# Graph layer on one core: the broadcast table of destination indices loaded as 16-bit instead of 32-bit numbers

## The chip, the cores and the metric

The kernel runs on one core of a Trainium2 chip. A core has five engines that run their own instruction streams and meet only at semaphores: TensorE (PE, with its weight loads shown as PEld), VectorE (DVE), ScalarE (ACT), GpSimd (POOL) and SyncE (SP), and 16 DMA engines that all queues share. The metric is the device time of one execution in microseconds (us); lower is better.

## The reference, cut to what matters

50,000 nodes with 160 features each, 50,000 edges sorted by destination node. For each edge the source node's features are gathered, put through a linear layer, multiplied by weights that a small network makes of the edge's own features, and added up per destination node. The sums turn the node's own linear layer by an angle; then comes a layer norm.

```python
h = silu(edge_scalars @ fc_w1 / sqrt(8));  weight = h @ fc_w2 / sqrt(64)
gs, gv = f_s[edge_src], f_v[edge_src]
m0a = gs * ys * w1_;                 m0b = sum(gv * yv[:, None, :], -1) * INV3 * w4_
m1a = gs[..., None] * yv[:, None, :] * w2_[..., None];  m1b = gv * ys[..., None] * w3_[..., None]
mid = segment_sum(edge_feat, edge_dst, num_segments=N) / sqrt(16)
angle = 0.1 * (mid_s @ lin3_w) / sqrt(96) * node_attr
return layernorm(x + cos(angle) * scfeat + sin(angle) * conv)
```

## The kernel before

Edges and nodes are padded to 392 tiles of 128 (`NT`), that is 196 pairs of tiles (`NPAIR`). The program has two stages, each a hand-written order per engine.

**Edge stage.** One step per pair. POOL gathers the source rows with an indirect DMA per tile (`gather`, L316), 644 bytes for each of 128 partitions, into a ring of 48 pairs. PE transposes them (L480) and runs the linear layers, ACT copies PSUM to SBUF, DVE forms the messages. `lin2` is applied per edge (L440, L442), and the rows of a tile that have the same destination are summed by a matmul with a 0/1 matrix `same_sb` (`combine`, L423 and L427). ACT copies the sums to a ring of 48 pairs, `comb_sb` (L553). POOL adds them to the table `acc` in HBM, one accumulating indirect DMA per tile (`scatter`, L329): 392 of them. Two semaphores, `scattered[0]` and `scattered[1]`, serve the even and the odd tile of a pair, and a scatter first waits until the scatter of the same parity in the pair before has landed (L328), so at most two are in flight and POOL's instructions behind that wait stand too.

POOL's order is written out: 120 gathers (`2 * AHEAD`), then for each tile one scatter and 0.73 gathers on average (272 over 372 scatters, L344), so one or two gathers stand among any two consecutive scatters' slots; the last 20 scatters have none.

**The table in question.** `same_sb` is made on DVE in L689, two instructions per pair. One takes a row of 256 destination indices (this tile's 128 and the next tile's, the same on all partitions), compares each with the partition's own destination index, `dst_f`, and multiplies by a weight matrix of fp32. The rows lie in `dstrow_sb`, in two rounds of 9 rows of 128 indices. One load per 4 pairs (`load_rows`, L542, on ACT's DMA queue) fills a round: each of the 128 partitions gets the same 9 x 128 indices of `dst_rows` from HBM. There are 49 loads. ACT issues load c after it has copied the last tile of the chunk before (L573), and DVE waits for it once in 4 pairs (L685).

```python
dstrow_sb = sb("dstrow_sb", [P, ROUNDS, 2 * CHUNK + 1, P], i32)
act.dma_start(dstrow_sb[:, c % ROUNDS, :, :], rows.to_broadcast([P, 2 * CHUNK + 1, P])
              ).then_inc(dstrow_in[c % ROUNDS], 16)
```

On the same ACT queue `load_scalars` (L535) brings 32 KB per chunk. On SP's queue, 50 stores of zeros to `acc` run in the first 125 us, and five loads of the node stage's inputs (L243, L255) go out between 892 us and 1133 us.

**Node stage.** When both `scattered` semaphores are full (L277), SP loads `acc` back and the node stage runs: `x_n` tiles, self connection on PE, angle, y and layer norm on POOL, DVE and ACT, stores on SP.

Of the kernel before, what the change touches and what calls it, by code (L numbers as in the profile page):

```python
# [6 lines left out]
P = 128  # L7
# [15 lines left out]
CHUNK = 4  # L23
ROUNDS = 2
# [26 lines left out]


def gnn_program(nc, xa, x_odd, x_last, src, dst, dst_rows, ea4, ea8t, constants, acc, out):
    fp32, i32 = mybir.dt.float32, mybir.dt.int32
    ALU, ACT = mybir.AluOpType, mybir.ActivationFunctionType
    NT = dst.shape[1]
    NPAIR = NT // 2
# [32 lines left out]
    with ExitStack() as ctx:  # L90
        def sb(name, shape, dt=fp32):
            return ctx.enter_context(nc.sbuf_tensor(name, shape, dt))
# [23 lines left out]
        row_sb = sb("row_sb", [P, NT], i32)  # L116
        dst_i = row_sb
        is_last = sb("is_last", [P, NT])
        dstrow_sb = sb("dstrow_sb", [P, ROUNDS, 2 * CHUNK + 1, P], i32)

        CS_COLUMNS = LOADED * BATCH * G * ROWA
        shared = sb("shared", [P, CS_COLUMNS + Y_RING * G * ROW])
# [811 lines left out]
def layouts(x, src, dst, edge_attr_4, edge_attr_8, node_vec1, sc_w0, sc_w1, lin1_w0, lin1_w1, fc_w1,  # L934
            fc_w2, lin2_w0, lin2_w1, lin3_w, tiles):

    n, e = x.shape[0], src.shape[0]
    rows = tiles * P
    f32 = np.float32
    xa = np.zeros((rows, ROWA), f32)  # L940
    xa[:n, 0], xa[:n, 1:1 + NV], xa[:n, 1 + NV:] = node_vec1[:, 0], x[:, NS:], x[:, :NS]
    src_p = np.zeros(rows, np.int32)
    src_p[:e] = src
    dst_p = np.full(rows, n, np.int32)
    dst_p[:e] = dst
    ea4 = np.zeros((rows, 4), f32)
    ea4[:e] = edge_attr_4
    ea8 = np.zeros((rows, EDGE_S), f32)
    ea8[:e] = edge_attr_8

    def by_component(w, rows_grouped, cols_grouped):

        u, c = w.shape
        m = np.zeros((u, 3, c, 3), f32)
        for d in range(3):
            m[:, d, :, d] = w
        if rows_grouped:
            m = m.transpose(1, 0, 2, 3).reshape(3 * u, c, 3)
        else:
            m = m.reshape(3 * u, c, 3)  # L960
        if cols_grouped:
            m = m.transpose(0, 2, 1)
        return np.ascontiguousarray(m.reshape(3 * u, 3 * c))

    lin2_a = np.zeros((P, NS + 1 + MU), f32)
    lin2_a[:NS, :NS] = lin2_w0[:NS]
    lin2_a[:NS, NS] = lin3_w[:NS, 0]
    lin2_a[NS:, NS + 1:] = lin2_w1[:NS]
    lin2_b = np.zeros((P, OUTW), f32)
    lin2_b[:NV, :NV] = by_component(lin2_w1[NS:], True, False)  # L970
    lin2_b[NV:, NV:ROW] = lin2_w0[NS:]
    lin2_b[NV:, ROW] = lin3_w[NS:, 0]
    sc_a = np.zeros((P, ROW), f32)
    sc_a[:NV, :NV] = by_component(sc_w1, False, False)
    sc_a[NV:, NV:] = sc_w0[:P - NV]
    lin1_a = np.zeros((P, ROW), f32)
    lin1_a[:NV, NS:] = by_component(lin1_w1, False, True)
    lin1_a[NV:, :NS] = lin1_w0[:P - NV]

    def two_tiles(w):  # L980

        m = np.zeros((2 * w.shape[0], 2 * w.shape[1]), f32)
        m[:w.shape[0], :w.shape[1]] = m[w.shape[0]:, w.shape[1]:] = w
        return m

    order = np.arange(P)
    values = {
        "fc_w1": two_tiles(fc_w1),
        "fc_w2": np.concatenate([fc_w2, fc_w2]),
        "lin1_a": lin1_a,  # L990
        "lin1_b": two_tiles(lin1_w0[P - NV:]),
        "lin2_a": lin2_a,
        "lin2_b": lin2_b,
        "sc_a": sc_a,
        "sc_b": np.concatenate([two_tiles(sc_w0[P - NV:])] * 2),
        "ident": np.eye(P, dtype=f32),
        "weight": np.concatenate([np.triu(np.ones((P, P))), np.full((P, P), HANDED)], axis=1).astype(f32),
    }
    constants = np.concatenate([np.pad(values[name], ((0, P - shape[0]), (0, 0)))
                                for name, shape in CONSTANTS.items()], axis=1)  # L1000
    return {
        "xa": xa,

        "x_odd": np.concatenate([xa[:, 1 + P:], xa[:, 1:1 + P], xa[:, :1]], axis=1),

        "x_last": np.ascontiguousarray(xa[:, 1 + P:]),
        "src": src_p.reshape(P, tiles),
        "dst": dst_p.reshape(P, tiles),
        "dst_rows": np.concatenate([dst_p.reshape(P, tiles).T, np.full((1, P), -1, np.int32)]),
        "ea4": ea4.reshape(P, tiles, 4),  # L1010
        "ea8t": np.ascontiguousarray(ea8.reshape(P, tiles // 2, 2, EDGE_S).transpose(1, 2, 3, 0)
                                     ).reshape(tiles // 2, 2 * EDGE_S, P),
        "constants": constants,
    }
# [21 lines left out]
```

How the kernel before makes its waits and increments, by code:

```python
def wait(eng, sem, count):  # L47
    if count > 0:
        eng.wait_ge(sem, count)
# [167 lines left out]
        @block.sync  # L218
        def _(sp):
            sp.dma_start(src_sb[:, :], src).then_inc(src_in, 16)
            sp.dma_start(constants_sb[:, :], constants).then_inc(consts, 16)
            sp.wait_ge(zeroed_tile, 1)
            for c in range(ZEROS):
                wait(sp, acc_zeroed[c % ZEROING], c // ZEROING * 16)
                sp.dma_start(acc_z[c, :, :], zeros[:, :]).then_inc(acc_zeroed[c % ZEROING], 16)
            for z in range(ZEROING):
                sp.wait_ge(acc_zeroed[z], 16 * len(range(z, ZEROS, ZEROING)))
            def ring_free(columns):
                pairs = min(NPAIR, NPAIR - X_RING + -(-columns // (2 * ROWA)))
                sp.wait_ge(xt_ready, pairs)
                sp.wait_ge(q_done, pairs)
# [1 line left out]
            def load_x_last(b):  # L236
                g, count = BATCHES[b]
                if b < LOADED:
                    ring_free((b + 1) * BATCH * G * (ROW - P))
                else:
                    over, groups = BATCHES[b - LOADED]
                    sp.wait_ge(xnt_ready, over + groups)
                sp.dma_start(xl_sb[:, b % LOADED, 0:count * P], batch_rows(x_last, b).rearrange("p j c -> p (j c)")
                             ).then_inc(xl_in[b % LOADED], 16)
# [19 lines left out]
            def store(s):  # L264
                sp.wait_ge(norm_done, s + 1)
                if s >= TAIL_FIRST:
                    sp.wait_ge(norm_pool, s + 1 - TAIL_FIRST)
                if s >= TAIL_MIDDLE:
```

## Time and profile before

| | us |
|---|---|
| median of 3 runs (lowest, highest) | 1580.86 (1576.93, 1584.43) |
| the profiled execution's own time | 1580.58 |
| its span, first to last instruction | 1578.8 |
| edge stage, to the last scatter | 0 to 1294 |
| node stage, from SP's first load of `acc` | 1296 to 1578.8 |

| engine | busy us | share of the span |
|---|---|---|
| POOL | 1293.4 | 82% |
| PE | 1284.8 | 81% |
| DVE | 932.0 | 59% |
| ACT | 816.2 | 52% |

How to read the rows: a timeline row gives the start, the duration, the engine, the line of the program, the operation and the tiles, and in brackets how long the engine stood idle before it and what ended that. A POOL row of an indirect DMA is the time in which POOL writes the descriptors; the transfer follows. POOL shows about 0.30 us between any two of these instructions, whatever they wait for, so only what is above 0.30 is a stall, and the releaser named beside 0.30 means nothing. Queue q0 in the DMA tables is POOL's own, q10 is ACT's, q1 is SP's, and q8 and q14 fetch instructions.

### The profile page before, as it was taken

How to read it: one execution, taken by the hardware profiler on the slowest of the kernel's cores; microseconds unless marked ns; L12 is line 12 of the kernel's file. 1: busy time of each engine (PE TensorE's matmuls, PEld its weight loads, DVE VectorE, ACT ScalarE, POOL GpSimd, SP SyncE). 2: the span in 40 equal slices, each digit the busy share in tenths (PEclk: the TensorE clock that was granted, in tenths of full speed). 3: DMA queues.
4: the chain of work that ended last, by engine and by line, in shares of the span. 5: the costliest groups of instructions: out<-in, count | busy, mean ns of one | idle time of the engine just before them, and what ended most of it. 6: DMA issues, size and time to landing. Idle time of an engine off the chain costs nothing. (4 is left out here: it accounts for less than half of the span.)

```text
span 1578.8 us, 28888 instructions
## 1 busy us (share of the span) xinstructions
PE 1284.8 (81%) x8524; PEld 1134.3 (72%) x8524; DVE 932.0 (59%) x4681; ACT 816.2 (52%) x1877; POOL 1293.4 (82%) x1054
## 2 busy tenths in 40 slices
PE   6999999999999777776777777777777828888884
PEld 5888888888888666666666666666666716777774
DVE  4777777777776444435444435344444407999998
ACT  3666666666665333333333333333333403988896
POOL 7777888878878877778888888778788769999997
PEclk9999999999999888888888888888888868999998
DMA  9994444444444444344444454444444449999984
GB/s 370 380 387 131 81 81 83 81 80 82 82 79 82 73 75 65 63 67 81 66 67 66 85 85 84 64 66 80 104 66 66 62 90 385 367 415 399 401 337 182
DMA packets 114761, 235.19 MB, mean 149 GB/s; under 512 B 17264, under 2 KB 77232, under 8 KB 111024
## 3 DMA queue, kind: packets, MB, share of 16 engines
q0 software_dynamic: 75264, 64.68, 28.8%
q1 hardware_dynamic: 27936, 136.82, 21.8%
q10 hardware_dynamic: 11408, 31.84, 6.0%
q8 instruction: 72, 1.18, 0.3%
q14 instruction: 81, 0.66, 0.1%
HBM read 135.88 MB, written 97.40 MB: 148 GB/s over the span
## 5 line engine op out<-in xcount | busy, mean ns | idle before, releaser
L329 POOL DMA_INDIRECT acc<-shared,row_sb x392 | 625.1, 1595 | 144.5 <-issue 97.5
L716 DVE TENSOR_TENSOR shared<-shared 128x192 f32<-128x192 f32 x196 | 70.4, 359 | 559.1 <-ACT shared L581 559.1
L480 PE MATMUL XTZ<-constants_sb,x_shared 128*128 128x128 f32 x588 | 118.9, 316 | 200.5 <-DMA x_shared<-x_odd,src_sb 194.9
L316 POOL DMA_INDIRECT x_shared<-xa,src_sb x196 | 201.5, 1028 | 60.5 <-issue 44.5
L316 POOL DMA_INDIRECT x_shared<-x_odd,src_sb x196 | 199.5, 1018 | 59.7 <-issue 48.8
L480 PEld LDWEIGHTS XTZ<-constants_sb,x_shared 128*128 128x128 f32 x588 | 66.7, 152 | 230.3 <-DMA x_shared<-x_odd,src_sb 216.5
L440 PE MATMUL OC<-constants_sb,shared 128*128 128x193 f32 x784 | 231.8, 382 | 0.0
L589 ACT COPY shared<-XTZ 128x384 f32<-128x384 f32 x196 | 93.7, 478 | 257.3 <-PE XTZ L480 257.3
L423 PE MATMUL OC<-shared 128*128 128x161 f32 x784 | 199.0, 339 | 2.8 <-ACT shared L553 2.1
L553 ACT ACTIVATE shared<-OC,is_last 128x161 f32<-128x161 f32 x392 | 154.9, 395 | 72.2 <-PE OC L427 35.6
L427 PE MATMUL OC<-shared 128*128 128x161 f32 x782 | 189.9, 328 | 0.0
L568 ACT COPY shared<-OC 128x386 f32<-128x386 f32 x196 | 94.3, 481 | 177.7 <-PE OC L442 177.7
L689 DVE SCALAR_TENSOR_TENSOR shared<-dstrow_sb,dst_f,constants_sb 128x256 f32<-128x256 int32 x392 | 173.3, 478 | 0.0
L619 ACT ACTIVATE shared<-shared,shift,rstd_mean 128x160 f32<-128x160 f32 x361 | 158.3, 513 | 17.1 <-DVE shift L861 17.0
L442 PEld LDWEIGHTS OC<-constants_sb,shared 128*128 128x128 f32 x784 | 165.6, 223 | 0.0
L442 PE MATMUL OC<-constants_sb,shared 128*128 128x97 f32 x784 | 160.1, 291 | 0.0
L468 PE MATMUL W<-constants_sb,shared 64*128 64x192 f32 x784 | 157.9, 351 | 0.0
L440 PEld LDWEIGHTS OC<-constants_sb,shared 128*128 128x128 f32 x784 | 147.8, 225 | 0.0
L427 PEld LDWEIGHTS OC<-shared 128*128 128x128 f32 x782 | 145.8, 214 | 0.0
L459 PE MATMUL FPT<-constants_sb,shared 128*128 128x160 f32 x784 | 141.3, 303 | 0.6 <-ACT shared L589 0.6
L423 PEld LDWEIGHTS OC<-shared 128*128 128x128 f32 x784 | 135.3, 216 | 4.2 <-issue 1.8
L383 POOL TENSOR_TENSOR shared<-shared,x_shared 128x640 f32<-128x640 f32 x98 | 129.7, 1324 | 0.0
(92 smaller groups left out, 2695.5 us busy)
## 6 DMA issues: line engine op xcount, KB each, us to landing
acc<-xnt_zeros SPq DMA_DIRECT2D x50, 644.0 KB, 6.7
out<-shared SPq DMA_DIRECT2D x97, 320.0 KB, 10.2
x_shared<-xa SPq DMA_DIRECT2D x13, 2254.0 KB, 11.1
shared<-acc SPq DMA_DIRECT2D x13, 2254.0 KB, 16.1
dstrow_sb<-dst_rows ACTq DMA_DIRECT2D x49, 576.0 KB, 4.2
acc<-shared,row_sb POOLq DMA_INDIRECT x392
x_shared<-x_last SPq DMA_DIRECT2D x13, 448.0 KB, 11.2
x_shared<-xa,src_sb POOLq DMA_INDIRECT x196, 3.0
```

The costliest lines, as they stand in the source:

```text
L316: pool.indirect_dma_start(out=x_sb[:, slot, j * ROWA:(j + 1) * ROWA], out_offset=None, in_=(xa, x_odd)[j], in_offset=bass.IndirectOffsetOn ...
L329: pool.indirect_dma_start(out=acc, out_offset=bass.IndirectOffsetOnAxis(ap=row_sb[:, t:t + 1], axis=0), in_=comb_sb[:, k % RING, j, :], in ...
L423: last = nc.tensor.matmul(out_rows, same_sb[:, e % SLOTS, j, 0:P], feat_sb[:, e % SLOTS, j, 0:ROWA], start=True, stop=t == 0)
L427: last = nc.tensor.matmul(out_rows, same_sb[:, b % SLOTS, i, P:2 * P], comb_sb[:, b % RING, i, :], start=False, stop=True)
L440: nc.tensor.matmul(OUT[:, o:o + OUTW], pt_sb[:, d % 2, (2 + j) * P:(3 + j) * P], lin2_b_sb[:, :], start=True, stop=False)
L442: last = nc.tensor.matmul(OUT[:, o + NV:o + OUTW], pt_sb[:, d % 2, j * P:(j + 1) * P], lin2_a_sb[:, :], start=False, stop=True)
L459: nc.tensor.matmul(F[:, j * ROW:(j + 1) * ROW], xt_sb[:, k % 2, j * P:(j + 1) * P], lin1_a_sb[:, :], start=j == 0, stop=False)
L468: last = nc.tensor.matmul(W[:, j, 0:NW], h_sb[j * NS:(j + 1) * NS, k % 2, :], fc_w2_sb[j * NS:(j + 1) * NS, :], start=True, stop=True)
L480: last = nc.tensor.transpose(XT[:, b * P:(b + 1) * P], x_sb[:, x_slot(a), column:column + P], ident_sb[:, :])
L553: nc.scalar.activation(comb_sb[:, e % RING, j, :], COMB[:, j * ROWA:(j + 1) * ROWA], ACT.Copy, scale=is_last[:, t:t + 1]).then_inc(comb_co ...
L619: last = nc.scalar.activation(y[:, j, :], y[:, j, :], ACT.Identity, bias=shift[:, k % STAGED, n:n + 1], scale=rstd_mean[:, k % STAGED, 0, ...
L689: last = nc.vector.scalar_tensor_tensor(same_sb[:, d % SLOTS, j, :], dstrow_sb[:, chunk % ROUNDS, r:r + 2, :].rearrange("p b e -> p (b e)" ...
```

## The change

The host hands over only the low 16 bits of each destination index, and the SBUF tile and its load are 16-bit. All indices are at most 50,000 and thus fit; the filler row of -1 becomes 65,535, which no index equals. The comparison L689 reads a 16-bit operand now; its output and its other operands stay fp32. A load moves 2304 bytes per partition instead of 4608, and `dstrow_sb` takes 4608 bytes of SBUF per partition instead of 9216. No instruction is added, removed or moved on any engine.

```diff
-    fp32, i32 = mybir.dt.float32, mybir.dt.int32
+    fp32, i32, u16 = mybir.dt.float32, mybir.dt.int32, mybir.dt.uint16
...
-        dstrow_sb = sb("dstrow_sb", [P, ROUNDS, 2 * CHUNK + 1, P], i32)
+        dstrow_sb = sb("dstrow_sb", [P, ROUNDS, 2 * CHUNK + 1, P], u16)
...
-        "dst_rows": np.concatenate([dst_p.reshape(P, tiles).T, np.full((1, P), -1, np.int32)]),
+        "dst_rows": np.ascontiguousarray(np.ascontiguousarray(np.concatenate([dst_p.reshape(P, tiles).T, np.full((1, P), -1, np.int32)])).view(np.uint16)[:, ::2]),
```

## Rows read from the trace of the kernel before

**Rows 1.** Busy time by stretch: PE, PEld, DVE, ACT, POOL, clock, DMA share, GB/s.

```profile
157.00:300.00 143.00, 143.00 (x1043) 127.63 (x1040) 102.62 (x535) 90.06 (x208) 116.33 (x85) 1.00 0.47 81
300.00:500.00 200.00, 200.00 (x1456) 178.24 (x1455) 142.91 (x748) 126.27 (x292) 159.63 (x117) 1.00 0.48 84
500.00:700.00 200.00, 147.04 (x873) 132.35 (x871) 87.53 (x456) 75.91 (x175) 159.13 (x118) 0.85 0.43 68
1296.00:1578.00 282.00, 226.56 (x1639) 188.20 (x1639) 249.53 (x1139) 219.06 (x503) 264.80 (x262) 0.95 0.89 356
```

**Rows 2.** POOL's instruction groups from 157 to 1296 us: busy, mean ns, idle before.

```profile
L329 POOL DMA_INDIRECT acc<-shared,row_sb x392 | 625.1, 1595 | 144.5 <-issue 97.5 <-DMA acc<-shared,row_sb 29.4 <-ACT shared L553 8.2
L316 POOL DMA_INDIRECT x_shared<-xa,src_sb x136 | 142.7, 1050 | 41.4 <-issue 27.4 <-DMA acc<-shared,row_sb 7.0 <-PE XTZ L480 5.2
L316 POOL DMA_INDIRECT x_shared<-x_odd,src_sb x137 | 142.1, 1037 | 41.8 <-issue 30.8 <-DMA acc<-shared,row_sb 7.9 <-ACT shared L553 3.0
```

**Rows 3.** Timeline from 1292 us, POOL, SP and DVE.

```profile
1292.37 1.55 POOL L329 DMA_INDIRECT acc<-shared,row_sb  x1 [0.30 <-issue]
1295.89 0.80 SPq L262 DMA_DIRECT2D shared<-acc  x2
...
1299.96 0.21 POOL L354 TENSOR_TENSOR angles<-shared,x_shared 128x8 f32<-128x8 f32 x1 [6.04 <-DMA shared<-acc]
```

**Rows 4.** POOL's timeline around 551 us, and the load of index rows on ACT's queue.

```profile
549.56 1.57 POOL L329 DMA_INDIRECT acc<-shared,row_sb  x1 [0.30 <-ACT shared L553]
551.44 1.56 POOL L329 DMA_INDIRECT acc<-shared,row_sb  x1 [0.31 <-issue]
553.30 1.02 POOL L316 DMA_INDIRECT x_shared<-x_odd,src_sb  x1 [0.30 <-issue]
555.60 1.57 POOL L329 DMA_INDIRECT acc<-shared,row_sb  x1 [1.28 <-DMA acc<-shared,row_sb]
...
550.56 0.35 ACTq L542 DMA_DIRECT2D dstrow_sb<-dst_rows  x1
```

**Rows 5.** DMA queues: 551.4 to 553.2 us, then 553.2 to 555.2 us.

```profile
q10 hardware_dynamic: 111, 0.51, 87.6%
...
q0 software_dynamic: 300, 0.22, 81.6%
q10 hardware_dynamic: 33, 0.08, 11.7%
```

**Rows 6.** POOL's timeline in the last scatters, with no gathers and no index loads.

```profile
1282.01 1.55 POOL L329 DMA_INDIRECT acc<-shared,row_sb  x1 [0.81 <-DMA acc<-shared,row_sb]
1283.87 1.55 POOL L329 DMA_INDIRECT acc<-shared,row_sb  x1 [0.31 <-issue]
1286.23 1.55 POOL L329 DMA_INDIRECT acc<-shared,row_sb  x1 [0.81 <-DMA acc<-shared,row_sb]
```

**Rows 7.** POOL's timeline: three more scatters behind an index load: first, longest, last.

```profile
227.69 1.78 POOL L329 DMA_INDIRECT acc<-shared,row_sb  x1 [1.11 <-DMA acc<-shared,row_sb]
...
326.04 1.57 POOL L329 DMA_INDIRECT acc<-shared,row_sb  x1 [2.34 <-DMA acc<-shared,row_sb]
...
1233.94 1.64 POOL L329 DMA_INDIRECT acc<-shared,row_sb  x1 [0.67 <-issue]
```

**Rows 8.** DMA issues from 500 to 1250 us: KB each, median us to landing.

```profile
dstrow_sb<-dst_rows ACTq DMA_DIRECT2D x23, 576.0 KB, 4.0
...
x_shared<-x_last SPq DMA_DIRECT2D x1, 320.0 KB, 3.3
x_shared<-x_last SPq DMA_DIRECT2D x1, 128.0 KB, 2.8
```

**Rows 9.** DVE's comparison, by form; and what DVE waits for, 500 to 1250 us.

```profile
L689 DVE SCALAR_TENSOR_TENSOR shared<-dstrow_sb,dst_f,constants_sb 128x256 f32<-128x256 int32 x392 | 173.3, 478 | 0.0
L733 DVE SCALAR_TENSOR_TENSOR shared<-shared,W 128x96 f32<-128x96 f32 x392 | 103.5, 305 | 0.0
...
DVE shared L716 <- ACT shared L581: 409.2, 93, 7.4
```

**Rows 10.** POOL stalls with another transfer: an instruction fetch (q8, 572 to 575.5 us), an SP load.

```profile
576.30 1.56 POOL L329 DMA_INDIRECT acc<-shared,row_sb  x1 [1.04 <-DMA acc<-shared,row_sb]
...
q8 instruction: 1, 0.02, 2.7%
...
1140.90 1.57 POOL L329 DMA_INDIRECT acc<-shared,row_sb  x1 [2.87 <-DMA acc<-shared,row_sb]
```

**Rows 11.** POOL's waits from 157 to 1252 us: us in total, times, longest.

```profile
POOL acc L329 <- DMA acc<-shared,row_sb: 23.5, 22, 2.9
POOL acc L329 <- ACT shared L553: 7.9, 23, 1.2
```

**Rows 12.** DMA queues from 549.2 to 550.6 us, when the 32 KB load (L535) is served.

```profile
q10 hardware_dynamic: 80, 0.03, 10.2%
```

## The prediction, made before the changed kernel ran

> **What bounds the kernel now.** I read the table of busy time by stretch first. It has three regimes [rows 1]. Up to 500 us PE is busy all the time. From 500 us on PE has 147 of 200 us while POOL still has 159, and in the node stage, 1296 to 1578 us, the DMA share is 0.89. So one would call the kernel bound by PE, then POOL, then DMA. The groups of POOL's instructions correct this [rows 2]. From 157 us, the start of the first scatter, to the last one POOL spends 625.1 + 142.7 + 142.1 = 909.9 us in indirect DMAs and 144.5 + 41.4 + 41.8 = 227.7 us in gaps before them. That makes 1137.6 us, the whole way from 157 to 1294 us. Its 392 + 136 + 137 = 665 gaps cost 0.30 us each whatever happens: 199.5 us. Only 28 us are real stalls. POOL is thus a serial chain through both regimes; PE's full busy time in the first one only uses up the lead of the 120 gathers. And the edge stage ends with POOL: the last scatter is issued at 1292.37, SP's load of `acc` follows at 1295.89, and the node stage's first instruction at 1299.96 [rows 3]. So a microsecond taken from POOL's stalls is a microsecond off the time, and nothing else in the edge stage is.
>
> **What the change touches on that chain.** No instruction moves. What shrinks is the transfer of 49 loads, 576 KB to 288 KB. Does POOL ever wait for one? Not by name. But a scatter waits for the landing of the scatter of the same parity before it, and all share the 16 DMA engines. The timeline shows one such case [rows 4]. The scatter at 549.56 ends at 551.13, the next of its parity starts at 555.60, 4.47 us later. In between stand one scatter and one gather, after which POOL could have started at 553.30 + 1.02 + 0.30 = 554.62. It lost 0.98 us. The index load was issued at 550.56. The DMA table then says who was served: from 551.4 to 553.2 there are 111 packets of ACT's queue and not one of POOL's queue; those come after [rows 5]. The price of a landing without such neighbours is in the last scatters: one ends at 1283.56 and the next of its parity starts at 1286.23, 2.67 us later [rows 6]. So the index load delayed the landing by 4.47 - 2.67 = 1.80 us. With one gather between, POOL has 1.56 + 1.02 + 3 x 0.30 = 3.48 us to fill, a margin of 3.48 - 2.67 = 0.81 us; with two gathers 2.1 us. A delay of 1.80 costs about 1 us at the one spacing, and nothing at the other.
>
> I went through all POOL gaps over 0.45 us and looked which queues had packets while the awaited scatter was under way. Twelve had packets of the index load. The first is at 227.69 (0.81 us above 0.30), the longest at 326.04 (2.04), the last at 1233.94 (0.37) [rows 7], and the others are 0.85, 0.89, 0.63, 0.98, 0.88, 0.92, 0.96, 0.83 and 0.70. Together 10.9 us. Some stand in the summary of waits under another name, since the longest "ACT shared L553" wait is 1.2 us [rows 11].
>
> **The size of the gain.** How much shorter is the blockade with half the bytes? Loads of other sizes say it: 128 KB land in 2.8 us, 320 KB in 3.3, 576 KB in 4.0 [rows 8]. On that line (1.2 us per 448 KB, 2.7 ns per KB) 288 KB take 0.8 us less. The delay goes from 1.80 to about 1.0 us, the margin is 0.8, and 0.2 us of a stall is left. Per stall the gain is the smaller of 0.8 and the stall: nine at 0.8, plus 0.63, 0.70 and 0.37, in all 7.2 + 1.7 = 8.9 us. The bounds: 0 if the delay is one of the load as such and not of its bytes; 10.9 us if all of the twelve go. I take 8.9, since rows 8 give a slope in bytes. What is late next in those places is nothing new: POOL goes on at its 0.30 us.
>
> The Trainium skill bears on this, page "DMA: Bandwidth & Descriptors", section "SWDGE vs HWDGE vs iDMA": it says that each DMA engine has 16 internal queues, of which software- and hardware-made descriptors feed different ones, and that the engine goes round them in turn, switching at packet boundaries. By that rule a scatter would stand behind a packet or two of the index load and not behind all. The stretch with 111 packets of one queue and none of the other speaks against it here [rows 5], though the trace doesn't tell when POOL's descriptors were ready. What it would do to the time is the first rival.
>
> **The rest of the change.** L689 reads 16-bit numbers. It takes 478 ns for 256 columns where the same operation takes 305 ns for 96, which is 1.08 ns per column [rows 9]. Its second input and its output remain fp32. If the narrower input halved the cost per column, it would take 0.34 us, if it doubled it, 0.75 us. Either way it changes DVE by at most 2 x 0.28 = 0.6 us per pair. In 157 to 500 us, DVE is busy 245.5 of 343 us [rows 1], and a pair takes POOL 1137.6 / 196 = 5.8 us, of which DVE would use 4.1 + 0.6 at most. After that DVE waits 409 us in 93 pairs for ACT [rows 9]. Cost and gain zero, hidden behind POOL's lead. I take an unchanged 478 ns. In the first 125 us two index loads fight with the stores of zeros; POOL is issuing its 120 gathers then and its scatters start at 157 us regardless: zero. The node stage has no index loads: zero. The 4608 bytes of SBUF that come free move other tiles' addresses: zero.
>
> The sum: 1580.58 - 8.9 = 1571.7 us for the profiled execution. The median of the runs shown is 0.3 us above it, so 1572.0 us, 0.56% faster.
>
> **Rival 1, the delay is not one of bytes, or the engines alternate.** If a load costs the scatter a fixed wait, the gain is 0. If a scatter stands behind one packet only, it is half a packet's time, and a packet of the load takes 0.876 x 16 x 1.8 us / 111 = 0.23 us [rows 5]: 12 x 0.11 = 1.4 us. So 1579 to 1581 us. For it: the first packet's latency is most of the 4.0 us of a load [rows 8]. Against it: rows 5.
>
> **Rival 2, the gain is made up of coincidences that fall differently.** Only 12 of 49 loads cost something, depending on which spacing they meet. There are other neighbours of the same kind. An instruction fetch costs 0.74 us at 576.30, an SP load 2.57 us at 1140.90 [rows 10]. POOL's clock of events moves once the first stall is gone, and a scatter that had its margin to spare meets another fetch. The fetches made ten stalls of 0.34 to 0.88 us before 1252 us in this trace; four more of them, or one more behind an SP load, take away 3 us: 1574 to 1577 us, within 0.5%.
>
> **Rival 3, slower: the rows of 2-byte numbers aren't joined.** Now a partition's 9 rows of 128 indices go as one packet of 4608 bytes. If the nine rows of 256 bytes became packets of their own, a load would be 1152 packets. The nearest row is the 32 KB load of the edge scalars, whose 64 packets of 512 bytes and 16 semaphore writes take 0.102 x 16 x 1.4 us / 80 = 0.029 us each [rows 12]: 1152 / 16 x 0.029 = 2.1 us per load. At the tight spacing a stall is then 1.3 us. Of 49 loads 54% meet the tight spacing (2 - 2 x 0.73), that is 26, of which 12 cost something now, a share of 0.46. So 12 x 1.3 = 16 us in place of 10.9: 1586 us. At 0.04 us a packet the blockade is 2.9 us and the wide spacing pays as well: 0.46 x 49 x (0.54 x 2.1 + 0.46 x 0.8) = 34 us, 1604 us. It counts as slower from about 0.031 us a packet. Against it: the 4-byte rows are joined (128 packets of 4608 bytes are 576 KB, and rows 5 have 111 + 33 packets of this queue with its semaphore writes), and nothing in the access pattern but the element's size is different.
>
> **How the numbers follow.** The forecast has 0.52, rival 1 0.16, rival 2 0.25, rival 3 0.07. A measurement of this kernel tells about 0.5% from no change, which is 7.9 us, so 1573.0 us is the edge, and the forecast lies only 1 us beyond it. Of its 0.52 I count 0.42 as faster by over 0.5%, and 0.03 come from rival 2 on the lucky side. Faster 0.45, same 0.48, slower 0.07. The range: the low end is 1580.9 - 10.9 = 1570.0, less 3 us for what runs of one kernel differ (1576.93 to 1584.43 around 1580.86), 1567; the high end takes in rivals 1 and 2, to 1582.
>
> **What would show it.** In the profile after: the last scatter at about 1283.5 us instead of 1292.4, and from there the same 286 us to the end. ACT's queue with about half the bytes and the same number of packets (128 per load), landing about 0.8 us earlier. The twelve stalls of POOL behind index loads gone or at 0.2 us, while those behind instruction fetches and SP's loads remain. POOL's gaps before scatters 144.5 down to about 136 us; L689 still about 478 ns. The prediction is wrong if landings of the load fall by less than 0.3 us, if stalls of 0.8 us behind index loads are still there, or if POOL's stalls fall and the last scatter does not come earlier by as much.

## The result, and the profile after

The changed kernel takes 1575.47 us in the median of 20 runs (1571.05 to 1583.59), the kernel before 1581.76 us in 20 runs beside it. The ratio is 0.9955, with a 95% interval of 0.9942 to 0.9968, which is 7.1 us; the two medians are 6.3 us apart. The profiled execution took 1574.12 us, 6.5 us less than that of before (1580.58).

The edge stage ends earlier. This is the timeline of the changed kernel there, to be laid beside [rows 3]:

```profile
1284.56 1.55 POOL L329 DMA_INDIRECT acc<-shared,row_sb  x1 [0.65 <-issue]
1288.23 0.80 SPq L262 DMA_DIRECT2D shared<-acc  x2
...
1292.28 0.21 POOL L354 TENSOR_TENSOR angles<-shared,x_shared 128x8 f32<-128x8 f32 x1 [6.16 <-DMA shared<-acc]
```

The last scatter starts 7.8 us earlier, at 1284.56 instead of 1292.37, and SP's first load of `acc` 7.7 us earlier. The span ends at 1572.3 instead of 1578.8, 6.5 us earlier, so the node stage gave back 1.2 us; the change doesn't touch it.

POOL's groups, from 157 us to the end of the edge stage (busy, mean ns, idle before; against [rows 2]):

```profile
L329 POOL DMA_INDIRECT acc<-shared,row_sb x392 | 627.0, 1600 | 135.6 <-issue 104.3 <-DMA acc<-shared,row_sb 15.2 <-ACT shared L553 11.2
L316 POOL DMA_INDIRECT x_shared<-xa,src_sb x136 | 142.3, 1046 | 41.4 <-issue 25.9 <-DMA acc<-shared,row_sb 8.5 <-PE XTZ L480 5.8
L316 POOL DMA_INDIRECT x_shared<-x_odd,src_sb x137 | 141.5, 1033 | 41.7 <-issue 29.2 <-DMA acc<-shared,row_sb 10.0 <-ACT shared L553 2.4
```

The idle time before the scatters went from 144.5 to 135.6 us, and nothing else moved by more than 2 us. The comparison on VectorE costs what it did [rows 9], and ACT's queue moves 45% fewer bytes in the same 11,408 packets (first a group of instructions, then the queue over the whole span, then the load: KB, median us to landing):

```profile
L689 DVE SCALAR_TENSOR_TENSOR shared<-dstrow_sb,dst_f,constants_sb 128x256 f32<-128x256 uint16 x392 | 173.2, 477 | 0.0
...
q10 hardware_dynamic: 11408, 17.39, 4.3%
...
dstrow_sb<-dst_rows ACTq DMA_DIRECT2D x49, 288.0 KB, 3.6
```

The same queue in the kernel before, and the load there:

```profile
q10 hardware_dynamic: 11408, 31.84, 6.0%
...
dstrow_sb<-dst_rows ACTq DMA_DIRECT2D x49, 576.0 KB, 4.2
```

A load lands 0.6 us earlier in the median, not 0.8. And stalls behind it remain. This one, in POOL's timeline of the changed kernel, has a load issued at 642.21:

```profile
641.21 1.62 POOL L329 DMA_INDIRECT acc<-shared,row_sb  x1 [0.30 <-issue]
643.13 1.02 POOL L316 DMA_INDIRECT x_shared<-x_odd,src_sb  x1 [0.30 <-issue]
644.46 1.57 POOL L329 DMA_INDIRECT acc<-shared,row_sb  x1 [0.30 <-issue]
646.90 1.60 POOL L329 DMA_INDIRECT acc<-shared,row_sb  x1 [0.87 <-DMA acc<-shared,row_sb]
```

From the end of the first scatter, 642.83, to the next of its parity are 4.07 us. Less the 2.67 us without neighbours [rows 6] that is a delay of 1.40 us. The same two scatters in the kernel before stood at 647.64 and 653.59, with an index load issued at 648.47:

```profile
647.64 1.57 POOL L329 DMA_INDIRECT acc<-shared,row_sb  x1 [0.30 <-issue]
...
653.59 1.56 POOL L329 DMA_INDIRECT acc<-shared,row_sb  x1 [1.18 <-DMA acc<-shared,row_sb]
```

From 649.21 to 653.59 are 4.38 us, a delay of 1.71 us. So half the bytes took 0.31 us off this delay, where 0.8 was expected. At two more scatters that stall behind a whole load, and nothing else, in both traces (before at 1002.87 and 1131.89) it took off 0.34 and 0.33 us. The scatter of [rows 4], at 555.60 before, hardly stalls any more (first line below); another, at 1092.54, stalls by 0.88 us behind a load although it had no stall before (second line):

```profile
551.24 1.57 POOL L329 DMA_INDIRECT acc<-shared,row_sb  x1 [0.35 <-issue]
...
1092.54 1.72 POOL L329 DMA_INDIRECT acc<-shared,row_sb  x1 [1.18 <-DMA acc<-shared,row_sb]
```

Counting every gap before a scatter that is over 0.1 us above 0.30, and asking whose packets were under way, the trace before has 12 stalls behind index loads with 10.9 us, the trace after 12 with 5.7 us. The sorting isn't clean: six of the twelve before (6.1 us) and five of the twelve after (1.7 us) had an instruction fetch under way too. With index packets alone they are 6 with 4.7 us and 7 with 4.0 us. Stalls behind instruction fetches without a counted index load went from 6.9 to 3.1 us in these two executions; the change can't be the reason other than by shifting which scatter meets which fetch.

### The profile page after: what moved, and what is told of

It is laid out like the page before. It is cut to its first block and busy times, and to the rows that moved or that the text cites. A ratio compares the mean times of both kernels' runs of the same rounds, so it can differ in the third digit from the quotient of the medians.

```text
span 1572.3 us, 28888 instructions
## 1 busy us (share of the span) xinstructions
PE 1270.3 (81%) x8524; PEld 1119.7 (71%) x8524; DVE 932.0 (59%) x4681; ACT 817.4 (52%) x1877; POOL 1294.7 (82%) x1054
## 3 DMA queue, kind: packets, MB, share of 16 engines
q10 hardware_dynamic: 11408, 17.39, 4.3%
## 5 line engine op out<-in xcount | busy, mean ns | idle before, releaser
L329 POOL DMA_INDIRECT acc<-shared,row_sb x392 | 627.0, 1600 | 135.6 <-issue 104.3
L716 DVE TENSOR_TENSOR shared<-shared 128x192 f32<-128x192 f32 x196 | 70.3, 359 | 549.8 <-ACT shared L581 549.8
L316 POOL DMA_INDIRECT x_shared<-x_odd,src_sb x196 | 199.0, 1016 | 59.7 <-issue 47.2
L440 PE MATMUL OC<-constants_sb,shared 128*128 128x193 f32 x784 | 227.6, 376 | 0.0
L689 DVE SCALAR_TENSOR_TENSOR shared<-dstrow_sb,dst_f,constants_sb 128x256 f32<-128x256 uint16 x392 | 173.2, 477 | 0.0
L442 PEld LDWEIGHTS OC<-constants_sb,shared 128*128 128x128 f32 x784 | 162.2, 219 | 0.0
L440 PEld LDWEIGHTS OC<-constants_sb,shared 128*128 128x128 f32 x784 | 144.4, 220 | 0.0
L427 PEld LDWEIGHTS OC<-shared 128*128 128x128 f32 x782 | 144.2, 212 | 0.0
L423 PEld LDWEIGHTS OC<-shared 128*128 128x128 f32 x784 | 133.5, 213 | 4.2 <-issue 1.8
```

Source lines behind the costliest of these rows:

```text
L316: pool.indirect_dma_start(out=x_sb[:, slot, j * ROWA:(j + 1) * ROWA], out_offset=None, in_=(xa, x_odd)[j], in_offset=bass.IndirectOffsetOn ...
L329: pool.indirect_dma_start(out=acc, out_offset=bass.IndirectOffsetOnAxis(ap=row_sb[:, t:t + 1], axis=0), in_=comb_sb[:, k % RING, j, :], in ...
L423: last = nc.tensor.matmul(out_rows, same_sb[:, e % SLOTS, j, 0:P], feat_sb[:, e % SLOTS, j, 0:ROWA], start=True, stop=t == 0)
L427: last = nc.tensor.matmul(out_rows, same_sb[:, b % SLOTS, i, P:2 * P], comb_sb[:, b % RING, i, :], start=False, stop=True)
L440: nc.tensor.matmul(OUT[:, o:o + OUTW], pt_sb[:, d % 2, (2 + j) * P:(3 + j) * P], lin2_b_sb[:, :], start=True, stop=False)
L442: last = nc.tensor.matmul(OUT[:, o + NV:o + OUTW], pt_sb[:, d % 2, j * P:(j + 1) * P], lin2_a_sb[:, :], start=False, stop=True)
```

## The experiments

Each ratio is against executions of the kernel before beside it, with 5 to 12 of the experiment's kernel and the 95% interval in brackets. "Idle" below is always the idle time before the 392 scatters, of which 392 x 0.30 = 118 us is there whatever happens.

**Same bytes as before, 16-bit comparison.** Each load brings 18 rows, of which nine are never read.

```diff
+LOADED_ROWS = 18
...
-        dstrow_sb = sb("dstrow_sb", [P, ROUNDS, 2 * CHUNK + 1, P], u16)
+        dstrow_sb = sb("dstrow_sb", [P, ROUNDS, LOADED_ROWS, P], u16)
...
-                rows = dst_rows[2 * c * CHUNK:2 * (c + 1) * CHUNK + 1, :].rearrange("(o j) e -> o j e", o=1)
+                rows = dst_rows[2 * c * CHUNK:2 * c * CHUNK + LOADED_ROWS, :].rearrange("(o j) e -> o j e", o=1)
```

> The changed kernel, but each load of index rows brings 18 rows instead of 9 (the second nine are never read), so that a load has the bytes of the kernel before (4608 per partition) while the comparison on VectorE still reads 16-bit numbers. Theory A (the gain is that a shorter burst of the index load delays the landing of the scatter that GpSimd waits for by less; a stall is the delay less a margin of 0.8 us): back at the kernel before, ratio 0.999 to 1.001, stalls of GpSimd behind index loads about 11 us in total. Rival B (it was the 16-bit operand on VectorE or the SBUF addresses): ratio 0.995 to 0.996 as for the changed kernel.

Measured: 1.0001 (0.9987 to 1.0016), idle 147.9 us. The stalls behind index loads are 15.2 us in 18 places, more than the 11 expected, and the ratio is as expected for theory A. The gain is gone with the bytes, so it wasn't the 16-bit operand. This kernel does not test the SBUF addresses: with 18 rows of 16-bit numbers `dstrow_sb` takes the 9216 bytes of before, and the other tiles lie where they lay then. Four scatters in flight, below, tests them.

**Twice as many loads, each of half the rows**, once with 32-bit and once with 16-bit indices. A load covers 2 pairs, in four rounds of tiles, issued two loads ahead.

```diff
+ROW_CHUNK = 2
+ROW_LEAD = 2
+ROW_ROUNDS = 4
...
-                    if (e + 1) % CHUNK == 0 and (e + 1) // CHUNK + 1 < CHUNKS and (e + 1) // CHUNK + 1 >= ROUNDS:
-                        load_rows((e + 1) // CHUNK + 1)
+                    if (e + 1) % ROW_CHUNK == 0 and ROW_ROUNDS <= (e + 1) // ROW_CHUNK + ROW_LEAD < NPAIR // ROW_CHUNK:
+                        load_rows((e + 1) // ROW_CHUNK + ROW_LEAD)
```

> The kernel before with 32-bit indices, but the index rows come in 98 loads of 5 rows (2560 bytes per partition) instead of 49 of 9 rows (4608 bytes): bursts nearly as short as the changed kernel's, and in total 11% more bytes than before. Theory A (length of one burst decides): each delay about 1.0 us, so stalls of 0.2 to 0.5 us, though twice as many places: 3 to 7 us in total in place of 11, ratio 0.995 to 0.998. Rival C (the total of bytes decides, by load on the DMA engines): ratio 1.000 to 1.002.

> The changed kernel with the index rows in 98 loads of 1280 bytes per partition instead of 49 of 2304. Theory A: a delay of 0.5 to 0.7 us is under the margin of 0.8, no stalls behind index loads are left, about 5 us less than the changed kernel: ratio 0.991 to 0.993. Rival C (total bytes): ratio 0.9955 to 0.996, as the changed kernel. If twice as many load issues cost ScalarE or the engines more than they save, above 0.996.

Measured: 0.9997 (0.9982 to 1.0011) with 32 bits and 0.9968 (0.9949 to 0.9987) with 16. Both miss theory A, and the intervals of both admit the rival, the total of bytes. But the traces point to another reason: there are 31 stalls behind index loads with 14.7 us in the one and 24 with 12.3 us in the other. Where a load of 1280 bytes per partition stalled POOL, it was still by 0.5 us on average. The packets became shorter, the blockade hardly.

**One load per pair**, 196 loads of 768 bytes per partition (the same edit with `ROW_CHUNK = 1`, eight rounds, issued four loads ahead).

> The changed kernel with one load of 3 index rows per pair: 196 loads of 128 packets of 768 bytes, 18.9 MB in total against 14.5. Theories P and L: four times as many places at nearly the same delay as before, some 24 us of stalls (0.12 us per load as with 98 loads), ratio 1.004 to 1.008. Theory C (total of bytes decides): 0.996 to 0.998.

Measured: 1.0004 (0.9988 to 1.0020), 37 stalls with 20.5 us. That is less than the 24 us expected, and the ratio is below the range given. Yet the total of bytes (19.3 MB for the index rows, against 28.9 before) would have made it 0.996 to 0.998, and that is outside the interval. Theory C falls here. (The expectation has 18.9 MB; 196 loads of 128 packets of 768 bytes are 19.3.)

What one load does is seen in the DMA queues of this kernel from 383.1 to 384.1 us and from 384.1 to 385.1 us (packets, MB, share of 16 engines):

```profile
q10 hardware_dynamic: 75, 0.05, 24.8%
...
q0 software_dynamic: 66, 0.04, 53.6%
q10 hardware_dynamic: 69, 0.05, 21.5%
```

In the first microsecond ACT's queue has 75 packets, one per 13 ns, which keep the 16 engines busy for a quarter of the time. POOL's queue has none, though a gather issued at 379.97 was due (half of this kernel's gathers land within 3.3 us), and POOL's packets come again in the second stretch. With 4608 bytes per packet it was 111 packets in 1.8 us at 87.6% [rows 5]. So it isn't that the engines are full.

**The load cut by partitions.** If the number of packets is what blocks, fewer partitions per load must help where fewer rows didn't. 64 partitions are loaded at the old place and 64 one pair later; in a second kernel 32 after each pair, with three rounds.

```diff
-                act.dma_start(dstrow_sb[:, c % ROUNDS, :, :], rows.to_broadcast([P, 2 * CHUNK + 1, P])
-                              ).then_inc(dstrow_in[c % ROUNDS], 16)
+                act.dma_start(dstrow_sb[part * n:(part + 1) * n, c % ROW_ROUNDS, :, :],
+                              rows.to_broadcast([n, 2 * CHUNK + 1, P])).then_inc(dstrow_in[c % ROW_ROUNDS], 16)
...
-                    if (e + 1) % CHUNK == 0 and (e + 1) // CHUNK + 1 < CHUNKS and (e + 1) // CHUNK + 1 >= ROUNDS:
-                        load_rows((e + 1) // CHUNK + 1)
+                    if (e + 1) % CHUNK < ROW_PARTS and ROW_ROUNDS <= (e + 1) // CHUNK + ROW_LEAD < CHUNKS:
+                        load_rows((e + 1) // CHUNK + ROW_LEAD, (e + 1) % CHUNK)
```

> The changed kernel, each load of index rows cut by partitions: 64 partitions after the chunk's last pair, the other 64 one pair later. 98 loads, each of 64 packets of 2304 bytes. The two kernels with 98 loads of 128 packets did not gain over their parents, so a load has a part that does not shrink with its bytes. Theory P (that part goes with the number of packets): half the delay, under the margin of 0.8 us, stalls behind index loads at most 2 us, ratio 0.992 to 0.993. Theory L (it is one of each load whatever its size): 12 us of stalls as with the 98 loads of 1280 bytes, ratio 0.996 to 0.998.

> The same cut in four: 196 loads of 32 partitions, one after each pair, three rounds of tiles so that each has two chunks of time. Theory P: no stalls behind index loads, ratio 0.991 to 0.993. Theory L: 196 x 0.12 us = 24 us of stalls, ratio 1.004 to 1.008.

Measured: 0.9920 (0.9901 to 0.9940) for two parts, 0.9916 (0.9894 to 0.9938) for four, idle 135.1 and 134.7 us. The ratios are those of theory P. The same number of loads (98 and 196), each of 128 packets, had given 0.9968 and 1.0004, with 11% and 33% more bytes in total. The stalls came to 6.9 and 5.6 us, where theory P said at most 2 and none; but 4.9 and 4.5 us of them stand at scatters that an SP load of the node stage's inputs hit as well, and with index packets alone there is one stall of 0.1 us and none. The profiled executions don't show the further gain in the idle time (135.1 and 134.7 us, against 135.6 in the changed kernel), because other stalls happen to be longer in them. That the cut gains something over the changed kernel rests on the ratios (0.9901 to 0.9940 against 0.9942 to 0.9968) and the medians (1571.89 and 1570.27 us against 1575.47).

**The cut with 32-bit indices.**

> The kernel before with 32-bit indices, each load cut by partitions into two, 64 partitions after the chunk's last pair and 64 one pair later: 98 loads of 64 packets of 4608 bytes. If the number of packets in a load is nearly all that counts (theory P), it is as good as the 16-bit kernel cut the same way: ratio 0.992 to 0.994, stalls behind index loads under 8 us. If the bytes count as well, as the step from the kernel before to the changed one says (5 us of stalls for half the bytes at the same 128 packets): 0.995 to 0.997. A whole loss of the cut's gain (1.000) would mean that bytes alone count.

Measured: 0.9985 (0.9968 to 1.0002). The middle is outside both ranges given, and the stalls behind index loads came to 13.5 us, 5.4 of them where an SP load was under way too. Bytes do count as well: with the same cut, 64 packets of 4608 bytes are worse than 64 of 2304 by more than the intervals. And with 32 bits a gain of the cut itself is not shown: its interval takes in 1, and it overlaps that of the 98 loads cut by rows (0.9982 to 1.0011). The groups of the scatter in the kernels cut into two, with 16 and then with 32 bits (their line is L332 there):

```profile
L332 POOL DMA_INDIRECT acc<-shared,row_sb x392 | 625.1, 1595 | 135.1 <-issue 100.6 <-ACT shared L557 12.4 <-DMA acc<-shared,row_sb 9.9
...
L332 POOL DMA_INDIRECT acc<-shared,row_sb x392 | 623.5, 1591 | 142.3 <-issue 102.8 <-DMA acc<-shared,row_sb 15.7 <-ACT shared L557 13.6
```

The table puts the kernels beside each other. The burst is the median time from the first packet of a load to the end of its last, after 200 us; stalls and bursts are worked out from the packet records of one execution each. "Of these alone" leaves out the stalls where an instruction fetch or an SP load was under way too. The blocked time is the time from the burst's first packet until POOL's queue again starts 26 packets per us, half of its mean (semaphore writes not counted), averaged over all bursts in steps of 0.3 us. In the 3 us before a burst it is never under 27.

| kernel | loads | packets x bytes | burst us | blocked us | stalls behind loads | of these alone | idle us | ratio |
|---|---|---|---|---|---|---|---|---|
| before | 49 | 128 x 4608 | 2.66 | 1.8 | 12, 10.9 us | 6, 4.7 us | 144.5 | 1 |
| 16 bits, 18 rows | 49 | 128 x 4608 | 2.66 | 1.8 | 18, 15.2 us | 12, 9.5 us | 147.9 | 1.0001 |
| changed kernel | 49 | 128 x 2304 | 2.18 | 1.2 | 12, 5.7 us | 7, 4.0 us | 135.6 | 0.9955 |
| 32 bits, 2 pairs | 98 | 128 x 2560 | 2.17 | 1.2 | 31, 14.7 us | 21, 10.5 us | 142.9 | 0.9997 |
| 16 bits, 2 pairs | 98 | 128 x 1280 | 2.04 | 0.9 | 24, 12.3 us | 15, 7.5 us | 142.3 | 0.9968 |
| 16 bits, 1 pair | 196 | 128 x 768 | 1.96 | 0.9 | 37, 20.5 us | 20, 10.4 us | 145.0 | 1.0004 |
| 32 bits, cut in 2 | 98 | 64 x 4608 | 1.78 | 0.9 | 12, 13.5 us | 3, 2.0 us | 142.3 | 0.9985 |
| 16 bits, cut in 2 | 98 | 64 x 2304 | 1.31 | 0.6 | 5, 6.9 us | 1, 0.1 us | 135.1 | 0.9920 |
| 16 bits, cut in 4 | 196 | 32 x 2304 | 0.77 | 0.3 | 5, 5.6 us | none | 134.7 | 0.9916 |

With 128 packets the burst goes from 1.96 to 2.17 us between 768 and 2560 bytes, and to 2.66 us at 4608: it hardly gets under 2.0 us, about 15 ns a packet, however small the packets here are. With 2304 bytes each, 128, 64 and 32 packets take 2.18, 1.31 and 0.77 us. The columns of one execution scatter by some microseconds (stalls of 10.9 and 15.2 us, alone of 4.7 and 9.5, for the same 49 loads of the same size), so they rank the kernels at best; the ratios weigh.

**Four scatters in flight.** Here the wait itself is made harmless. Four semaphores in turn, and four sets of spare rows, so that no two scatters under way write the same row of `acc`.

```diff
-            pool.iota(spare_row[:, :], pattern=[[0, NPAIR], [P, 2]], base=NODES, channel_multiplier=1).then_inc(prep, 1)
+            pool.iota(spare_row[:, :], pattern=[[0, NT // IN_FLIGHT], [P, IN_FLIGHT]], base=NODES, channel_multiplier=1).then_inc(prep, 1)
...
-                if k > 0:
-                    pool.wait_ge(scattered[j], 16 * k)
+                wait(pool, scattered[t % IN_FLIGHT], 16 * (t // IN_FLIGHT))
```

> The changed kernel with four scatters allowed in flight instead of two: four semaphores in turn and four sets of spare rows, so that a scatter waits for the landing of the fourth one before it. Theory A with GpSimd as a serial chain: all of its stalls on landings go, whoever delays them (19 us in the trace after, 28 before): 1574 - 19 = 1555 us, ratio 0.983. Rival D (GpSimd's stalls are not what sets the edge stage's end, or PE becomes late): ratio 0.993 or more.

> The kernel before, 32-bit indices, with four scatters allowed in flight. If the whole worth of the 16-bit rows runs through the landings that GpSimd waits for, it is worth nothing here: same ratio as the 16-bit kernel with four in flight, 0.9837, within 0.0015. If part of it runs otherwise (writing of descriptors, PE, VectorE): 0.986 to 0.988.

Measured: 0.9837 (0.9812 to 0.9861), 1556.52 us, with 16 bits, and 0.9815 (0.9793 to 0.9837), 1555.74 us, with 32. The scatter's groups, 16 bits first, then 32, and the last scatters' timeline of the 16-bit one:

```profile
L329 POOL DMA_INDIRECT acc<-shared,row_sb x392 | 626.0, 1597 | 119.4 <-issue 95.0 <-ACT shared L554 11.0 <-DMA acc<-shared,row_sb 8.2
...
L329 POOL DMA_INDIRECT acc<-shared,row_sb x392 | 626.3, 1598 | 119.4 <-issue 97.5 <-ACT shared L554 8.2 <-DMA acc<-shared,row_sb 7.0
```

```profile
1264.17 1.55 POOL L329 DMA_INDIRECT acc<-shared,row_sb  x1 [0.30 <-issue]
1266.03 1.55 POOL L329 DMA_INDIRECT acc<-shared,row_sb  x1 [0.30 <-issue]
1269.52 0.80 SPq L263 DMA_DIRECT2D shared<-acc  x2
```

No gap above 0.32 us is left before any of POOL's DMAs behind the first scatter, and idle is 119.4 us in both. The stalls taken away, 144.5 - 119.4 = 25.1 us, are what the time fell by (24 to 28 us in the medians). That is the serial chain. And with the stalls gone no worth of the 16-bit rows is left to be seen: the two intervals overlap, and the 32-bit kernel is the lower of the two, by 0.8 us in the medians and further down than the 0.0015 expected. The 0.986 to 0.988 of a gain that runs otherwise lies outside its interval. So the worth of the change ran through the landings that POOL waits for, as far as five executions of each tell. That also speaks against the SBUF addresses: `dstrow_sb` has 4608 bytes in the one and 9216 in the other.

**Both together**, four in flight and the load cut in four:

> The changed kernel with both: four scatters in flight and loads of index rows in four parts. With four in flight no wait for a landing was left, so shorter blockades can give nothing more: ratio 0.982 to 0.984, as with four in flight alone. If the blockades also cost in another way (gathers that reach PE late), 0.980 or less.

Measured: 0.9824 (0.9807 to 0.9841), 1553.65 us, as expected. The blockades cost in no other way that this can tell. It has the lowest median of all kernels here, 1.8% below the kernel before by the ratio, though not apart from the other two with four in flight.

## Why the prediction was right, and where it was off

Range and direction held: 1575.47 us lies in 1567 to 1582. The forecast of 1572.0 was 3.5 us too low. Some 0.9 us of that is that the kernel before itself stands at 1581.76 in the longer series; in the difference it is 8.9 us forecast and 6.3 measured in the medians, or 7.1 by the ratio. The gain of 0.45% by the ratio is just under the 0.5% that the chances were set by, so "same", given 0.48, is what came.

- **What bounds the kernel**: right. POOL's chain sets the edge stage's end; the last scatter came 7.8 us earlier for 8.9 us less idle before the scatters (POOL's instructions took 0.9 us more, its first scatter was 0.3 us later). Four in flight shows it at three times the size.
- **The way**: right. Index load, scatter's landing, POOL's wait. The 18-row kernel gives the gain back and four in flight leaves nothing of it to be seen.
- **The step that was mis-sized** is "how much shorter is the blockade with half the bytes". The prediction took 2.7 ns per KB from the line through the index load and a 128 KB load [rows 8]. That one was a single issue of 2.8 us; in the trace after the same load landed in 2.2 us. Measured, the median of 49 landings fell by 0.6 us, and the delay at the three scatters that still stall behind a whole load, and nothing else, in both traces by 0.31 to 0.34 us instead of 0.8. The stalls behind index loads came to 5.7 us, where 10.9 - 8.9 = 2.0 was expected to be left: a gain of 5.2 us. One of the prediction's own signs of being wrong came: stalls of 0.8 us behind index loads are still there, at 245.23 (0.92, beside a fetch) and at 1092.54 (0.88).
- **A second weakness** is the sorting of stalls. Six of the twelve that the prediction priced in full as the index load's had an instruction fetch under way too, 6.1 of the 10.9 us, and a thirteenth, at 1031.92 (0.76), that it left to the fetches had 50 packets of the index load. How much of those was the load's is not shown. That the gain as a whole comes with the bytes is shown by the 18-row kernel's runs, not by this count.
- **Why**: a load has a part that goes with its 128 packets. Rival 1 said that the delay might not be one of bytes, and that is half true. Its reason (a fixed wait per load) is not: with 16 bits, the cut in two and in four makes more loads and shorter blockades, and the time falls.
- **Rival 2**, coincidences: in these two executions they were worth 3.8 us the lucky way, with fewer stalls behind fetches. So it is luck that the idle time in the trace after is less by just the forecast 8.9 us: at most 5.2 us of it stand at index loads, and part of those may be chance too, with fetches beside them. How much the change is worth, only the 20 runs on each side tell.
- **Rival 3**, rows not joined: no. There are 11,408 packets before and after.
- **The rest at zero** (L689, SBUF addresses): nothing speaks against it. L689 took 477 ns, and the 18-row kernel's 1.0001 has the 16-bit operand and no gain. The addresses are tested by four in flight alone, where kernels with either size of `dstrow_sb` take the same time within the intervals.

In the kernel with 768-byte packets POOL's queue had no packet for a microsecond in which the engines were three quarters idle. The Trainium skill's rule (page "DMA: Bandwidth & Descriptors", section "SWDGE vs HWDGE vs iDMA") is that an engine goes round its queues at packet boundaries, and the prediction took from it that a scatter stands behind a packet or two of the load. That step is not safe: the same section lets a packet hold up to 64 descriptors, so it need not be what the profile counts as one. The 128 packets of a load, shared out evenly, are 8 per engine. If these are one packet of the rule, the rule would keep POOL's queue out until all 8 are done, idle or not, and that would fit the traces; if each is one, it gives no reason for the gap. The packet records don't tell the engines apart, and no run tells whether POOL's packets wait by this rule, for their descriptors, for memory or for something that both queues share. That stays open.

## What to carry to other kernels

Where an engine waits for its own transfers, look which other queue's packets fall between issue and landing; the summary of waits doesn't name them. Here a broadcast load to 128 partitions blocked by its number of packets as well as its bytes. With 16-bit rows, cutting it by partitions over time helped (0.992) where cutting it by rows only added loads (0.9968 and 1.0004); with 32-bit rows neither cut showed a gain. Before shaving the neighbour, ask whether the wait can be given slack: two more scatters in flight brought 1.6 to 1.8%, about four times the whole change, and left nothing for the change to gain.

## What the runs showed of the hardware that was not expected

- 128 small packets of ACT's queue took about 2 us to be started, 15 to 16 ns each in the median, whether they had 768, 1280 or 2304 bytes. For the first 0.9 to 1.2 us of that POOL's queue started less than half of its usual packets, at the lowest 3 to 11 per us of a mean of 52.
- POOL's indirect DMAs have two lengths. In the trace before 91 of 665 take 80 to 320 ns longer than the usual 1572 or 1016 ns, 16 us in all. Of these 85% overlap the VectorE addition L695, and 15% of the others do; in the trace after it is 94% and 14%. But the instructions next to it tie in nearly as well (the comparison L689 with 82% and 25% before, L700 with 75% and 13%), so which of them it is, if any, isn't told. L716, a product of the same 192 columns, shows no such tie (15% and 28%). It was not tried by an experiment.
- VectorE's comparison with a 16-bit first input and fp32 for the rest took 477 ns, with a 32-bit one 478 ns.
